# Attention of all groups moved behind one common preparation, with the intermediates kept in device memory

## The reference

```python
x = x + L0(gn(x))  # 9 taps: patch * cf[b,c,tap] * sf[b,tap,pixel]; cf from a small MLP on the mean,
                   # sf from a 1x1 convolution, both normalised over the 9 taps
x = x + L1(gn(x))  # v * sigmoid(q . mean(k)), v, q, k from 1x1 convolutions
x = x + L2(gn(x))  # 3x3 convolution, 64 to 64 channels, weights in {-1, 0, 1}, plus bias
# L3: attention over the 3136 pixels of each image, 16 channels of Q and K, 64 of V
S = jnp.einsum('bkp,bkq->bpq', Q, K)
A = jax.nn.softmax(S, axis=-1)
x = x + jnp.einsum('bpq,bvq->bvp', A, V)
```

## Time and profile before

| | |
|---|---|
| time, median of 3 runs | 1786.28 us (1779.34 to 1786.63) |
| the profiled execution | 1779.75 us, its span 1778.0 us |
| PE busy | 1627.6 us, 92% of the span |
| ACT, DVE, POOL busy | 69%, 68%, 62% |
| mean granted clock of PE | 0.971 of full |

### The profile page before, as it was taken

One profiled execution on the slowest core, in us unless ns is written; L12 is line 12 of the kernel. 1 busy time (PEld: TensorE's weight loads), 2 busy tenths in 40 slices (PEclk: granted clock), 3 DMA queues, 4 the chain that ended last, 5 costly groups with the idle time before them and its releaser, 6 DMA issues.

```text
span 1778.0 us, 29563 instructions
## 1 busy us (share of the span) xinstructions
PE 1627.6 (92%) x10912; PEld 831.6 (47%) x10912; DVE 1211.9 (68%) x2299; ACT 1220.2 (69%) x2308; POOL 1110.1 (62%) x886
## 2 busy tenths in 40 slices
PE   5987899999989799999998879999999788999997
PEld 4454444444546344444443634444444454444442
DVE  5846777775574877777476488777738558777760
ACT  2045899998513689999832378999972337899994
POOL 2720478888761067888966016888887402788888
PEclk9989999999999999999999899999999899999998
DMA  2004000000000400000000040000000012000000
GB/s 90 1 1 77 15 6 7 7 7 6 11 1 1 91 2 6 7 7 7 11 6 0 3 89 1 6 7 12 7 6 6 0 30 26 5 9 7 7 7 11
DMA packets 12385, 26.87 MB, mean 15 GB/s; under 512 B 4560, under 2 KB 8912, under 8 KB 11728
## 3 DMA queue, kind: packets, MB, share of 16 engines
q1 hardware_dynamic: 12240, 24.99, 5.9%
HBM read 8.80 MB, written 6.42 MB: 9 GB/s over the span
## 4 chain that ended last, share of the span: by engine, by line
PE 65%; DVE 15%; ACT 7%; issue 4%; POOL 4%; POOLq 0%; DVEq 0%; ACTq 0%
PE PS L1333 24%; PE PS L1291 11%; PE PS L1261 11%; PE PS L1233 6%; DVE nmt L692 6%; PE PS L1192 4%; DVE nmt L685 3%; ACT Pb L962 3%; ACT PS L917 2%; POOL accP L1096 1%; PE PS L1224 1%; PE PS L1177 1%; PE PS L1225 1%; PE PS L1144 1%; PE PS L1305 1%
## 5 line engine op out<-in xcount | busy, mean ns | idle before, releaser
L685 DVE TENSOR_REDUCE nmt<-PS 128x1 f32<-128x448 f32 x1176 | 681.3, 618 | 211.7 <-PE PS L1261 208.0
L1096 POOL TENSOR_TENSOR accP<-accP,Pb 128x512 f32<-128x512 f32 (+1 forms) x532 | 677.7, 1274 | 128.2 <-ACT Pb L962 79.2
L962 ACT ACTIVATE Pb<-PS 128x896 f32<-128x896 f32 (+1 forms) x700 | 636.8, 915 | 123.3 <-PE PS L1291 115.7
L1333 PE MATMUL PS<-Pb,VT 128*64 128x448 f32 x2800 | 661.3, 545 | 4.3 <-ACT Pb L962 3.6
L1261 PE MATMUL PS<-Ka,Qa 96*64 96x448 bf16 x2888 | 497.7, 355 | 23.5 <-ACT PS L917 10.8
L1291 PE MATMUL PS<-Qa,Ka 99*64 99x448 bf16 x2744 | 492.1, 354 | 3.0 <-ACT Pb L962 2.5
L917 ACT ACTIVATE PS<-PS,nmt 128x448 f32<-128x448 f32 x588 | 357.0, 607 | 33.1 <-DVE nmt L692 27.3
L1261 PEld LDWEIGHTS PS<-Ka,Qa 96*64 96x64 bf16 x2888 | 165.9, 110 | 269.5 <-issue 115.9
L1291 PEld LDWEIGHTS PS<-Qa,Ka 99*64 99x64 bf16 x2744 | 168.7, 110 | 242.5 <-issue 188.4
L1333 PEld LDWEIGHTS PS<-Pb,VT 128*64 128x64 f32 x2800 | 195.7, 137 | 104.4 <-ACT Pb L962 28.6
L1089 POOL TENSOR_TENSOR accQ<-Pb 128x512 f32<-128x512 f32 x28 | 35.5, 1270 | 219.4 <-ACT Pb L962 219.4
(11 more groups left out here) (153 smaller groups left out, 1590.8 us busy)
## 6 DMA issues: line engine op xcount, KB each, us to landing
xin<-in_x SPq DMA_DIRECT2D x4, 1568.0 KB, 11.0
out<-xw SPq DMA_DIRECT2D x28, 224.0 KB, 1.9
Qa<-parts SPq DMA_DIRECT2D x24, 168.0 KB, 6.9
Ka<-parts SPq DMA_DIRECT2D x24, 112.0 KB, 3.7
Ka<-parts SPq DMA_DIRECT2D x24, 84.0 KB, 2.6
Qa<-mpt SPq DMA_DIRECT2D x96, 1.3 KB
wz<-in_weights SPq DMA_DIRECT2D x1, 829.0 KB, 7.8
Qa<-parts SPq DMA_DIRECT2D x24, 28.0 KB, 2.0
```

Of the source, the lines that this page charges most:

```text
L685: nc.vector.reduce_max(nmt[:, target % 2, b, t:t + 1], PS[0:BLK, bank, 0:CH], X, negate=True).then_inc(mx_free, 1)
L962: nc.scalar.activation(Pb[0:r, j % PSLOTS, :, :], PS[0:r, 2 * (k % 2):2 * (k % 2) + 2, 0:CH], ACT.Exp).then_inc(exp_done, 1)
L1096: nc.gpsimd.tensor_tensor((accQ if j < TO_ACCP else accP)[0:r, :, REST:CH], (accQ if j <= TO_ACCP else accP)[0:r, :, REST:CH], Pb[0:r, j % ...
L1333: last = mm(PS[C * h:C * h + C, OB, 0:CH], VT[:, j, C * h:C * h + C], Pb[:, j % PSLOTS, h, :], start=(j == 0), stop=(j == NQ - 1))
```

## The change

1. `group(g)` ends after the projections and values. Its `xw`, `parts` and `VT` are stored to three new tensors in device memory, `saved_x`, `saved_parts`, `saved_v` (1.6, 1.2 and 1.6 MB a group).
2. A new function `attention()` follows on each engine after all four groups. First maxima are taken once; then 28 superblocks run as one pipeline, `TILES_AT` spanning all of them, so that each superblock from 1 to 25 carries 49 tiles.
3. Q, K and V of a group are loaded back from device memory, 12 DMAs of 200 KB and one of 1.6 MB, into one of two sets of buffers (`Qs`, `Ks`, `Vs`): `Qa`, `Ka`, `VT` or the memory of `xin`, `xnp`, `xnf`. The set for group g+1 is requested after step 18 of superblock 7g+1. Chunks of `xw` are loaded back one by one after the store of the chunk that lay there.
4. The front of group g+1 no longer stands in superblock 6; it stands between the chunks of group g's convolution. The convolution uses 5 banks instead of 7 (`CONV_BANKS`), its second input lies in `xnf` instead of `xnp`, and `SF` lies in `Ka`.
5. The value products stand between the Q/K products; their copies to `VT` go from ACT to DVE.
6. The rows of ones in `Ka` are no longer written by POOL at the start, but ahead of the attention.

```diff
-        xnf = sb("xnf", [P, HW])
+        xnf = sb("xnf", [P, NQ * P])
-        SF = xnf[0:3 * PITCH, 0:HW // 2].bitcast(BF16)
+        SF = Ka[0:3 * PITCH, 0, :]
+        Qs = [xin[:, :].bitcast(BF16).rearrange("p (h n) -> p h n", h=2), Qa[:, :, :]]
+        Ks = [xnp[:, 0:HW].bitcast(BF16).rearrange("p (h n) -> p h n", h=2), Ka[:, :, :]]
+        Vs = [xnf[:, :].rearrange("p (a b) -> p a b", b=P), VT[:, :, :]]
...
+            def prepare(g):
+                if g < GROUPS - 1:
+                    sp.wait_ge(pool_step, POOL_STEPS * len(UNITS) * (g + 1) + 2)
+                    sp.dma_start(xin[:, :], x[g + 1]).then_inc(x_loaded, 16)
+                else:
+                    sp.wait_ge(parts_saved, 16)
+                    sp.wait_ge(conv_ready, NJ * g + 1)
+                    load_keys_queries(0)
+                sp.wait_ge(l2_done, NJ * (g + 1))
+                sp.dma_start(saved_x[g], xw[:, :]).then_inc(x_saved, 16)
+                sp.wait_ge(part_l, NJ * (g + 1))
+                sp.dma_start(saved_parts[g], parts[:, :, :]).then_inc(parts_saved, 16)
+                sp.wait_ge(v_ready, NJ * (g + 1))
+                sp.dma_start(saved_v[g], VT[:, :, :]).then_inc(v_saved, 16)
+            def attend(sidx):
+                g, s = divmod(sidx, NJ)
+                if sidx:
+                    c = slice((sidx - 1) % NJ * CH, ((sidx - 1) % NJ + 1) * CH)
+                    sp.wait_ge(fin_done, sidx + 1)
+                    sp.dma_start(out[(sidx - 1) // NJ][:, c], xw[:, c]).then_inc(stored, 16)
+                if sidx < SBS - 1:
+                    sp.wait_ge(mp_turned, sidx + 1)
+                    load_max_rows(sidx + 1)
+                if s == 1 and g < GROUPS - 1:
...
+                    load_keys_queries(g + 1)
+                    load_values(g + 1)
+                if sidx and sidx + NJ <= SBS:
+                    sp.wait_ge(stored, 16 * sidx)
+                    sp.dma_start(xw[:, c], saved_x[(sidx - 1) // NJ + 1][:, c]).then_inc(x_back, 16)
...
@@ tensor, group @@
+                for j in range(NJ):
+                    convolve(j, min(j + 2, NJ))
+                    if more:
+                        if j == 0:
+                            pair_mean(g + 1, 0, front)
+                        elif j == 1:
+                            front_mid(g + 1)
+                            for i in range(NJ):
+                                front_spatial_filter(g + 1, i)
+                        elif j == 2:
+                            front_channel_filter(g + 1)
+                        else:
+                            for i in range(2 * j - 6, min(2 * j - 4, NJ)):
+                                front_transpose(g + 1, i)
...
@@ vector, group @@
+                if more:
+                    front_stats(g + 1, range(0, 5))
+                low_filter_part(0)
+                low_filter_part(1)
+                if more:
+                    front_stats(g + 1, range(5, 6))
...
+                add_filtered(2)
+                if more:
+                    front_parts(g + 1)
+                    front_centre(g + 1)
+                add_filtered(3)
...
+                    if j:
+                        low_part(dve, g, j - 1)
+                        values_out(j - 1)
@@ gpsimd, attention @@
+                pool.wait_ge(conv_ready, NJ * (GROUPS - 1) + 1)
+                pool.wait_ge(gn_rstd[3], GROUPS)
+                nc.gpsimd.memset(Ks[0][KROWS:KROWS + 3, :, :], 1.0).then_inc(key_ones, 1)
...
-                for s in range(NJ):
-                    superblock(s)
+                for sidx in range(SBS):
+                    superblock(sidx)
```

More of the change, by code:

```diff
@@ L107, in take @@
         return bank, last
-    weight = [0.5 if k % NQ in (FINISH_STEP - 1,) else 1.0 for k in range(NQ * NJ)]
+    weight = [0.5 if k % NQ in (FINISH_STEP - 1,) else 1.0 for k in range(NQ * SBS)]
     at = {}
-    for s in range(1, NJ):
+    for s in range(1, SBS):
         end = NQ * (s - 1) + SPLIT_STEP + 1
@@ L120, in plan_banks @@
     reduced = summed = 0
-    for k in range(NQ * (NJ - 1)):
+    for k in range(NQ * (SBS - 1)):
         s, j = divmod(k, NQ)
@@ L200, in build @@
         ve = sb("ve", [P, 1])
-        rstd = sb("rstd", [P, 1])
-        nb = sb("nb", [P, 1])
+        rstd = [sb(f"rstd{i}", [P, 1]) for i in range(2)]
+        nb = [sb(f"nb{i}", [P, 1]) for i in range(2)]
         pooled = sb("pooled", [P, 2])
@@ L376, in _ @@
                 sp.dma_start(dst, src).then_inc(taps_loaded, 16)
-            sp.sem_inc(stored, 16)
-            for loaded in (q_first, k_first, k_rest, q_rest):
-                sp.sem_inc(loaded, 16)
             for first in (ocopy, d_ready, recip, fin_done):
@@ L439, in low_part @@
+            for g in range(0, GROUPS):
+                prepare(g)
+            load_values(0)
+            sp.wait_ge(x_saved, 16 * GROUPS)
+            sp.wait_ge(xn_ready[3], NJ * GROUPS)
+            sp.dma_start(xw[:, :], saved_x[0]).then_inc(x_back, 16)
+            for sidx in range(SBS + 1):
+                attend(sidx)
+            sp.wait_ge(stored, 16 * SBS)
         def low_part(dve, g, j):
@@ L490, in mean_var @@
             def mean_var(g, layer, last):
[L491 removed]
+                link(last)
                 nc.vector.memset(idle[:, :], 0.0)
@@ L509, in stats, with front_stats @@
                 bias(g, layer, small)
-            def front_stats(g):
-                n[0] = 0
-                dve.wait_ge(x_loaded, 16 * g + 16)
-                for i in range(NJ - 1):
-                    chunk_stats(xin, i)
-                mean_var(g, 0, chunk_stats(xin, NJ - 1))
+            def front_stats(g, chunks):
+                for i in chunks:
+                    if i == 0:
+                        dve.wait_ge(x_loaded, 16 * g + 16)
+                    last = chunk_stats(xin, i)
+                if i == NJ - 1:
+                    mean_var(g, 0, last)
             def front_bias(g):
                 bias(g, 0, front)
-                nc.vector.tensor_tensor(pooled[:, 0:1], front[:, DIFF_COL:DIFF_COL + 1], rstd[:, :],
+                nc.vector.tensor_tensor(pooled[:, 0:1], front[:, DIFF_COL:DIFF_COL + 1], rstd[1][:, :],
                                         ALU.mult).then_inc(pooled_ready, 1)
@@ L826, in _ @@
             group(GROUPS - 1, False)
+            attention()
         @block.scalar
@@ L896, in group @@
                 act.wait_ge(gn_nb[3], g + 1)
-                for loaded in (q_first, k_first, k_rest, q_rest):
-                    act.wait_ge(loaded, 16 * (SPREADS * g + 1))
+                if g:
+                    act.wait_ge(parts_saved, 16 * g)
                 for j in range(NJ + 2):
@@ new lines, in group, with value_columns @@
+                pair_stats(3, 5)
+                def value_columns(i):
+                    if i >= 2:
+                        pe.wait_ge(v_ready, NJ * g + i - 1)
+                    if i == 1 and more:
+                        pe.wait_ge(SF_ready, NJ * (g + 2))
+                    for j in range(4 * i, min(4 * i + 4, NQ)):
+                        r = key_rows(j)
+                        last = mm(PS[0:r, VALUE_BANKS[i % 2], (j % 4) * P:(j % 4 + 1) * P], xnf[:, j * QC:j * QC + r],
+                                  wcol("wv3"), start=True, stop=True)
+                    last.then_inc(v_ps, 1)
@@ L1383, in group @@
                     tile_of(NJ - 1, 0, NJ - 1, NJ - 1)
-                pe.wait_ge(mrow, g + 1)
-                pe.wait_ge(q_rest, 16 * (SPREADS * (g + 1) + 1))
-                for j in range(2):
+                pe.wait_ge(mrow, 1)
+                pe.wait_ge(key_ones, 2)
+                for k in range(2):
                     for h in range(2):
-                        scores(j, 0, h)
-                for s in range(NJ):
-                    superblock(s)
-                if more:
-                    pe.wait_ge(yvar_ready, g + 2)
-                denominators(NJ * g + NJ - 1, 7)
+                        scores(k, h)
+                for sidx in range(SBS):
+                    superblock(sidx)
+                denominators(SBS - 1, 7)
             pair_mean(0, 0, front)
```

536 lines of the change are left out of this document (251 added, 285 removed).

## The result

The changed kernel takes 1724.74 us (median of four executions, 1718.54 to 1730.94) against 1782.81 for the kernel before (four, 1778.82 to 1786.63): ratio 0.9674, 95% interval 0.9621 to 0.9728. The forecast was 1705, range 1690 to 1727. Executions of either kernel come at two levels, 1719 and 1730 for the one, 1779 and 1786 for the other. The two levels turn out to be a part of the answer.

What follows compares the result with a forecast made beforehand. PE was taken to set the ordinary superblocks (busy 155.9 of 157.4 us), with nothing beside the first maxima. -90.3 - 24.7 - 7.8 - 1.6 + 8.4 + 39 = -77 gave span 1701, execution 1703, stated 1705; range 1690 to 1727.

Steps and rivals of the forecast that it cites:

- rival 1: Convolution: clock stays low through the front and the chunks after it, 19.4 per front; 19 us more, 1724; chance 0.12.
- start: Start of the kernel: PE's first product no longer waits for POOL to write the ones of `Ka`; 1.6 us gained.
- First maxima, superblocks, handing over: Attention: three of four first maxima removed, 90.3 us gained; joint superblocks become ordinary, 24.7; handing over falls away, 7.8.
- Rival 4: Attention: the pipeline joins nothing and only the first maxima go; 32 us more, 1737; chance 0.04.
- The front in the convolution: Convolution: the next group's front adds 13 us, with filter 5.5, clock 2.5 and DVE wait 0.5; 39 for three.
- The plain reading: Convolution: an engine occupied without a gap stays at 2.4 GHz; front 10.5 us, sum 84; not followed in the forecast.
- Rival 2: Convolution: the front isn't overlapped and costs 28.2 instead of 13; 46 us more, 1751; chance 0.05.
- DMA: Attention: a load set takes 28 us, needed within 47; no cost taken, upper bound 3 us each time.
- rival 3: Attention: loads run one after another and starve the pipeline, 110 us a set; 189 more, 1894, slower; chance 0.05.
- Projections: Projections: value products hide each other's drain, 1.75 us a chunk; PE takes 13.9; cost 2.1 each, 8.4 for four.

Runs made afterwards that it cites:

- e8: Changed kernel with the 49 maximum tiles of superblocks 7, 14 and 21 all taken at the last step of the superblock before; 1803.60 us, ratio 1.0132.
- e3: Changed kernel with the front of groups 1 to 3 left out, these groups using group 0's; 1678.10 us, ratio 0.9409.
- e10: Changed kernel with the spatial filter's products taken twice in groups 1 to 3, into the same places; 1752.76 us, ratio 0.9831.
- e6: Changed kernel with each set of 13 loads followed by a second, nearly equal set to places nobody reads; 1744.30 us, ratio 0.9808.
- e9: Changed kernel with the Q and K product of every chunk taken twice into the same bank; 1746.28 us, ratio 0.9798.
- e4: Changed kernel with DVE's last two value copies of the projections ahead of the last low parts; 1718.71 us, ratio 0.9637.
- e5: The repeat: changed kernel once more with no edit, on another chip; 1719.61 us, ratio 0.9659, profiled span 1717.7.
- e1: Changed kernel with the spatial filter in pieces between blocks of nine convolution products instead of one run; 1719.57 us, ratio 0.9639.
- e2: Changed kernel with 16 filler products in L0 and 18 ahead of the convolution, in each group; 1723.4 us, ratio 0.9659.

## Why the prediction was right, and where it was 20 us off

The sign, the mechanism and most of the size held: the gain is 58 us by the medians (1782.8 to 1724.7), where the sum had 77. By profiled executions of the same, lower level it is 60 (1778.0 to 1717.7); the 50 to the profile after compares a lower level with an upper one. That 1724.7 lies in the range is in part luck. The forecast's own terms gave 1692 to 1716, and neither 1724.7 nor the repeat's 1719.6 is in that; the range reached to 1727 to take in rival 1 at 1724, and rival 1 didn't occur. What filled its place was a miss of 12 us in the projections, for which the range had no term, and two of the first four timings (1729.8, 1730.9) lie above 1727. Stage by stage, all four groups together, over the forecast's span of 1701:

| | forecast | after, 1728.0 | repeat, 1717.7 |
|---|---|---|---|
| projections | 69.8 | +11.9 | +12.1 |
| convolution with the front | 175.9 | +7.8 | +1.7 |
| L1 | 80.0 | +5.4 | +0.1 |
| L0 | 193.5 | +1.2 | +1.9 |
| first maxima, start | 30.1, 39.8 | +1.0 | +0.9 |
| attention | 1098 | 0 | 0 |

**First maxima, superblocks, handing over: right.** One stretch is left, 31.0. The joints are ordinary superblocks, as e8 shows from the other side: taken at once, the 49 tiles of a joint cost PE 30.3 us alone, what the earlier trace rows show for the first maxima before (30.1), and 28 us of superblocks per joint. Taken together, first maxima, superblocks and handing over were to gain 123 us, of which some 36 are the front leaving superblock 6 (44.9 - 33.0, three times); the 84 us that e8 loses are nearly all of the rest. So what the change gains in the attention comes from the spreading over other work, not from the loads and stores that make it possible. Rival 4 is out.

**The front in the convolution: right, 13.7 to 14.0 for 13.** e3 takes it out alone. The filter and its clock were 5.5 + 2.5 and are 8.8; DVE's late parts were 0.5 and are 0.19. Moving the front was by itself no gain: it cost 11.9 in superblock 6 and costs 13.7 to 14.0 here; it makes room for the joints. The plain reading of the Trainium skill, *TensorE: Matmul & The Clock Gate*, section "Part 1: The HAM clock gate", by which sustained work keeps the clock high, does not hold for products of 18 columns: in e10 it falls under them and stays low until they end. The forecast's weighing of row over rule stands. Rival 1, the clock low through the whole filter and two blocks (19.4), didn't occur, but at the upper level the front costs 15.6. The remark against rival 1 that the clock rose within the first nine products misreads the trace before: these are low throughout (3.73), and it rose in the second nine (2.29). Rival 2 is out: 13.7, not 28.

**DMA: right, and rival 3 measured.** A set takes 26.2 us for the 28 that the rate of `xin` gave, and nothing waits. The agreement hides two rates, 135 and 307 GB/s. Rival 3's mechanism is real, as e6 shows: 47.6 us for two sets costs 8.2 us per joint, the first of it a wait of 6.0. The slack behind one set is some 16 us, from its landing at 722.7 to the time at which PE ran out of work in e6, 739.0. That is 42 us behind the first issue; the forecast's limit of 47 was some 5 too generous, without harm at 26.2. (The 24 loads that it set against rival 3 were 2.4 MB, not 1.8.) The 35 us that the forecast estimated by the Trainium skill, *DMA: Bandwidth & Descriptors*, section "Anatomy of one DMA", for a strict sequence is above the 26.2. That section of the Trainium skill gives the fit for DMAs issued by GpSimd, and these are issued by SyncE. Nor was it a strict sequence: 13 loads were issued in 8.2 us and lay over one another.

**Projections: the step that failed.** The forecast said that each product has "some 0.2 of drain that the next one hides: 1.75" a chunk. The chunk takes 1.98 in the profile after and 1.98 to 1.99 in the repeat: 0.90 from the Q and K product to the values and 1.09 back, 0.97 and 1.16 being their whole lengths. So only 0.07 is hidden where the kind changes, while a second product of the same kind adds 0.75 for a length of 0.97 (e9), 0.22 hidden. e9 also confirms that PE sets the pace. Seven chunks make 1.6 us; PE's own part of the stage is 15.3 us in the repeat (from its first product at 297.99 to the end of the last) for the forecast's 13.9. (In that 13.9 the 2.4 for the low level don't follow from the rows named: 4.79 less three times 0.96 is 1.9.) The second part is at the end: the forecast gave DVE's last copy 0.5 behind PE, and the next stage begins 1.9 behind it, since DVE has a copy and a low part still ahead of the last one (e4 takes 1.2 to 1.3 of that back). 1.4 and 1.4 are nearly the 2.9 of a stage, 12 us for four. That DVE "has room" was too much as well: it is busy 1.75 a chunk, exactly the chunk of the forecast, so that with the drain hidden it would have had no slack left. I had looked at DVE's busy sum for the stage and not at what one chunk asks of it.

**The clock's level: a term that was missing.** The forecast took 6 us for the spread of runs and subtracted between the two levels of before, 7 to 9 us apart. The changed kernel's levels are 10 to 12 apart. The front in the convolution may account for the difference, since that stage moves by 1.9; no profile of the upper level of before is there to show it. The first four timings fell two and two on either level, so their median, 1724.7, is between them; e5's four were all lower, 1719.6. Against that the forecast is 15 us off; by the span it is 16.7, 12.1 of it projections. What decides the level of an execution isn't settled: e9's six executions on one chip fell on both. Shown is only where the time goes, L1 and convolution, and that the granted clock is lower there.

## What to carry to other kernels

When a stage moves from a waiting engine to a busy one, write out one steady period for every engine of it, with start-to-start distances between products of different kinds and not their durations less an assumed drain; the busy time of the engine that comes second there says how far the period can shrink. Where thin products are put between dense ones, don't price them all at the high clock: here 56 records cost 7.1 instead of 5.5 and the blocks behind them 1.7, and 56 more cost 10.5. Look at how an execution's granted clock differs from stage to stage before you credit an edit with a few us: a repeat of the unedited kernel showed here that e1 and e4, which looked like 5 and 6 us, were worth 0.0 and 0.9. A large set of loads ahead of small urgent ones in the same queue is hidden only up to a slack, and that can be measured by doubling the set.

## What the runs showed of the hardware

- The granted clock fell while PE was occupied without a gap by products of 18 columns: 1.00 for the first 4.0 us of 112 such records, 0.50 to 0.52 for the rest (e10). It was back by the second block of nine products of 448 columns (2.69 us after the filter in the profile after, 2.25 in the repeat, where a block at the low level takes 3.7). Each thin product also brings a weight load (PEld busy for 9.80 of the last 9.80 us), and no run separates the two.
- Half the clock can cost nearly nothing: the first maxima ran at a mean clock of 0.56 in 31.0 us, before at 1.00 in 30.1, where PE also had the value products. The 49 tiles of a joint in e8 took 30.3 at 0.57. DVE is busy 27 of these, and PE waits for it and ACT. A low clock is worth mending only where PE is what the others wait for.
- The same L0, instruction for instruction, took 48.6 at a granted clock of 0.93 (repeat) and 46.9 at 0.96 (e9), with an edit in another stage alone; the mean clock doesn't fix its time, for in e1 it took 48.0 at 0.96. Fillers (e2) moved the low stretches and didn't remove them.
- Maximum rows of 1.3 KB, issued at 733.48, let PE go on at 745.0 only, with a set of 4 MB and its twin ahead of them in the queue, the last of which landed at 744.8 (e6).
- Loads of 196 KB into 16 partitions each kept the 16 DMA engines busy (share 1.02) at 135 GB/s; the end of the set, mostly the one load of 1.6 MB, went at 307 with a share of 0.75 (profile after).
